# A selective-scan kernel whose channel picks contract 32 rows instead of 128

## What is computed

```python
def _mamba(x, in_proj_w, conv_w, conv_b, x_proj_w, dt_proj_w, dt_proj_b, A_log, Dvec, out_proj_w):
    xz = x @ in_proj_w.T
    xs, z = jnp.split(xz, 2, axis=-1)          # 128 inner channels each
    ...                                        # short convolution over tokens, silu
    dbc = xs @ x_proj_w.T
    dt = jax.nn.softplus(dbc[..., :DT_RANK] @ dt_proj_w.T + dt_proj_b)
    Bm = dbc[..., DT_RANK:DT_RANK + D_STATE]   # 16 states
    Cm = dbc[..., DT_RANK + D_STATE:]
    A = -jnp.exp(A_log)
    dA = jnp.exp(dt[..., None] * A)
    dBu = dt[..., None] * Bm[:, :, None, :] * xs[..., None]
    ...                                        # hs: h = dA * h + dBu along the tokens
    y = jnp.einsum('blds,bls->bld', hs, Cm) + xs * Dvec
    y = y * jax.nn.silu(z)
    return y @ out_proj_w.T
```

## Time and profile before

| | us |
|---|---|
| median of 3 runs | 6328.1 |
| lowest and highest | 6323.62 and 6338.3 |
| profiled execution, its own time | 6333.79 |
| its span, first to last instruction | 6332.1 |
| busy: PE | 4712.9 (74%) |
| busy: DVE | 4177.0 (66%) |
| busy: POOL | 3262.2 (52%) |
| busy: ACT | 3214.8 (51%) |
| granted TensorE clock, mean | 0.905 |

### The profile page before, as it was taken

One profiled execution on the slowest core, in us unless ns is written; L12 is line 12 of the kernel. 1 busy time (PEld: TensorE's weight loads), 2 busy tenths in 40 slices (PEclk: granted clock), 3 DMA queues, 4 the chain that ended last, 5 costly groups with the idle time before them and its releaser, 6 DMA issues. The chain is left out here.

```text
span 6332.1 us, 72725 instructions
## 1 busy us (share of the span) xinstructions
PE 4712.9 (74%) x22126; PEld 1875.5 (30%) x22126; DVE 4177.0 (66%) x6781; ACT 3214.8 (51%) x6875; POOL 3262.2 (52%) x2921
## 2 busy tenths in 40 slices
PE   4766887668876688766977669776797767977669
PEld 2322433214322143221432224322243223332233
DVE  3599635995359944599445994459834699346983
ACT  2555454554545555454554545445454454645545
POOL 1399203992149811498115980159701697017970
PEclk9899788997889988899888998889888998989989
DMA  3356133660335504365033650346413464135631
GB/s 86 82 139 140 26 78 74 147 144 14 88 85 138 135 10 94 79 149 124 18 91 91 139 117 21 87 99 146 102 25 83 108 141 98 28 80 122 140 85 28
DMA packets 205745, 582.54 MB, mean 92 GB/s; under 512 B 75652, under 2 KB 117892, under 8 KB 205188
## 3 DMA queue, kind: packets, MB, share of 16 engines
q1 hardware_dynamic: 205316, 577.47, 39.8%
HBM read 511.20 MB, written 66.20 MB: 91 GB/s over the span
## 5 line engine op out<-in xcount | busy, mean ns | idle before, releaser
L1065 POOL TENSOR_TENSOR hc<-hs,cb 128x448 f32<-128x448 f32 x1792 | 2029.2, 1146 | 329.1 <-DVE hs L1002 329.0
L1002 DVE TENSOR_TENSOR_SCAN hs<-dA,state,ps 128x448 f32<-128x448 f32 x1792 | 2036.4, 1137 | 13.8 <-ACT dA L965 13.8
L991 DVE TENSOR_TENSOR ps<-ps,bb 128x448 f32<-128x448 f32 x1792 | 1095.4, 611 | 309.4 <-PE ps L902 309.1
L952 ACT ACTIVATE state<-hs 128x1 f32<-128x1 f32 x1768 | 357.0, 202 | 1358.0 <-DVE hs L1002 1358.0
L902 PE MATMUL ps<-hx,pick 128*128 128x448 bf16 x2688 | 702.8, 376 | 413.2 <-DVE hs L1002 343.2
L902 PE MATMUL ps<-dux,pick 128*128 128x448 bf16 x2688 | 687.7, 370 | 364.6 <-DVE hs L1002 360.5
L537 POOL TENSOR_TENSOR sp<-hx,dA 128x448 f32<-128x448 f32 x56 | 59.9, 1069 | 1399.2 <-ACT dA L673 1399.2
L1412 DVE SCALAR_TENSOR_TENSOR dA<-ps,be,hs 128x448 f32<-128x448 f32 x224 | 153.2, 684 | 764.2 <-PE ps L1267 677.2
L1346 ACT ACTIVATE rz<-ps,be 128x448 f32<-128x448 f32 x896 | 540.8, 629 | 168.2 <-PE ps L1254 167.1
L1254 PE MATMUL ps<-u,we1s 128*128 128x448 bf16 x2688 | 614.3, 364 | 4.2 <-PEq L1093 4.2
L887 PE MATMUL ps<-hc,gather 128*32 128x448 f32 x3584 | 466.5, 594 | 144.9 <-POOL hc L1065 144.9
(11 more groups left out here) (186 smaller groups left out, 6697.6 us busy)
## 6 DMA issues: line engine op xcount, KB each, us to landing
rz<-dt_scratch SPq DMA_DIRECT2D x112, 896.0 KB, 6.4
x_all<-dt_scratch SPq DMA_DIRECT2D x112, 896.0 KB, 10.0
xn<-dt_scratch SPq DMA_DIRECT2D x112, 896.0 KB, 13.6
dtb<-dt_scratch SPq DMA_DIRECT2D x112, 896.0 KB, 13.3
zs<-h_scratch SPq DMA_DIRECT2D x174, 290.0 KB, 6.0
dt_scratch<-dtx SPq DMA_DIRECT2D x112, 224.0 KB, 1.9
h_scratch<-dA SPq DMA_DIRECT2D x168, 112.0 KB
u<-h_scratch SPq DMA_DIRECT2D x56, 336.0 KB, 4.1
```

Source lines behind the costliest of these rows:

```text
L952: A.activation(state[:, k % 2, i:i + 1], hs[:, n % RH, at:at + 1], ACT.Copy).then_inc(st_ok, 1)
L991: V.tensor_tensor(bank, bank, bb[:, k % 2, :], ALU.mult).then_inc(bu_ok, 1)
L1002: V.tensor_tensor_scan(rev(hs[:, n % RH, :], d), rev(dA[:, n % RA, :], d), rev(ps[BU[n % 3]][:, 0:CH], d), state[:, d, i:i + 1], ALU.mult, ...
L1065: P.tensor_tensor(hc[:, n % RC, :], hs[:, n % RH, :], cb[:, k % 2, :], ALU.mult).then_inc(hc_ok, 1)
```

## The change

A pick matmul now reads only the 32 lanes that hold its group's channels: stationary `pick[at, i % 4, :]` and moving `dux[k % 2][at, a, :]` with `at` the lanes 32 j to 32 j + 31, j = i // 4. Within such a block of 32 lanes the matrix depends on q = i % 4 alone, so four matrices take the place of sixteen, and each holds the same 32-row pattern in all four blocks. Results, output lanes, columns (128 stationary, 448 moving) and the number of matmuls stay as they were.

```diff
-        pick = sb("pick", [128, DS, 128], BF16)
+        pick8 = sb("pick8", [128, 4, 8])
+        pick = sb("pick", [128, 4, 128], BF16)
...
-                for i in range(DS):
-                    then(V.tensor_copy(pick[:, i, :].rearrange("p (s e) -> p s e", e=8),
-                                       ident[:, :].rearrange("p (j e q) -> p j q e", j=4, q=4)[:, i // 4, i % 4, :]
-                                       .unsqueeze(1).to_broadcast([128, DS, 8])))
+                for q in range(4):
+                    then(V.reduce_sum(pick8[:, q, :], ident[:, :].rearrange("p (j e q) -> p q e j", j=4, q=4)[:, q], axis=AX.X))
+                    then(V.tensor_copy(pick[:, q, :].rearrange("p (s e) -> p s e", e=8),
+                                       pick8[:, q, :].unsqueeze(1).to_broadcast([128, DS, 8])))
...
                         for a in range(3):
-                            last = nc.tensor.matmul(ps[BU[n % 3]][:, 0:CH], pick[:, i, :], top(dux[k % 2][:, a, :]),
+                            at = slice(32 * (i // 4), 32 * (i // 4) + 32)
+                            last = nc.tensor.matmul(ps[BU[n % 3]][:, 0:CH], pick[at, i % 4, :], top(dux[k % 2][at, a, :]),
                                                     start=(a == 0), stop=(a == 2))
```

## The result

The changed kernel takes 7308.6 us in the median of four runs (7298.0 to 7311.0), against 6333.2 before: a ratio of 1.154, 95% interval 1.152 to 1.156. It is slower by 975 us, clearly, and beyond the 7190 us at which the range ended. The direction and the place were forecast; the forecast growth, some 670 us, was a third too small.

What follows compares the result with a forecast made beforehand. VectorE sets the pace, TensorE is late at a few places. At 1.2 GHz a step grows from 27.1 to 34.0 us: 6328.1 + 707 (clock) - 44 (clock coming back) + 8 (start-up) = 6999, say 7000 us; range 6570 to 7190.

Steps and rivals of the forecast that it cites:

- the picks' own duration: Pick matmuls in the scan loop: contracting 32 rows instead of 128 makes them no shorter, 0 us.
- The preparation: VectorE's copies into the pick tile before the loop: any saving hides under GpSimd's power, so nothing gained.
- The clock: TensorE in the scan loop: empty rows don't count as activity, so 1.2 GHz through most of it, +707 us.
- The allowance for the clock coming back over skip and gather: Once per step: a quarter of the 1.58 us loss taken off in 112 steps, 44 us.
- A gather alone: Three per step at 1.2 GHz: the product behind the picks that follow is 0.89 us late each time.
- A preparation: dt, B, C matmuls between two pick groups, three per step: the product is 0.96 us late at 1.2 GHz.
- Skip and gather: Behind the gate, once per step: the product is 2.79 us late at 1.2 GHz, against 1.21 before.
- The upper bound: Every place at 1.2 GHz, picks after skip included, plus uncovered weight loads: 35.4 us a step, 7190 us.
- The sign that the prediction named: If the loop is far over 480 us: picks slow by themselves, over 1.4 us for three, from loads or drains.
- Same: Rival: busy time counts, not rows, so the loop's clock stays at 1.00; 6325 to 6330 us; 7%.
- faster: Rival: 32-row picks come out earlier, telling after skip and after the second gather; 45 us, 6283 us; 2%.
- Slower with the clock up: Rival: weight loads into the same 32 rows wait for the running matmul; 6373 to 6395 us; 3%.

Runs made afterwards that it cites:

- e1: Changed kernel plus useless 128-row filler matmuls on TensorE at the start of each image and behind pick groups without gather or preparation; 7122.9 us, ratio 1.123.
- e5: Changed kernel plus more 128-row fillers: bursts of 42 and 14 per image, 1 to 4 behind every other pick group; 6468.8 us, ratio 1.022.
- e2: Changed kernel with the fillers of e1, same number, places and columns, but over 32 rows instead of 128; 7444.5 us, ratio 1.175.
- e8: Kernel before, with its sixteen pick matrices and old preparation, only the picks reading 32 rows in every step; 7290.1 us, ratio 1.151.
- e4: Kernel before with its sixteen matrices, picks reading 32 rows in six of fourteen steps and 128 in the others; 6827.8 us, ratio 1.078.
- e3: Picks over 64 rows with eight pick matrices, instead of 32 rows with four as in the changed kernel; 7298.1 us, ratio 1.153 to the kernel before.
- e6: Kernel before, with 128-row picks, plus the same 128-row fillers as e5; 6278.3 us, ratio 0.991.

## Why the prediction was wrong in size and right in kind

**What bounds, and the picks' own duration: right.** In the stretches of e1 and e5 at 1.00 three narrow picks take 0.76 us, as full ones do (0.77). The Trainium skill's sentence "K=32 single mm = same time as K=128" (TensorE: Matmul & The Clock Gate, Why this matters for your kernels) holds here. Something that could run beside the narrow picks existed all the same, on other rows and into another bank: the fillers of e2.

**The preparation: right**, by e8, the first scan at 282 us in both, and the idle time of 8.21 us.

**The clock: right.** 0.51 over the block, within the "0.5 to 0.6" named, and the wait of the product went where it was looked for. The inference from the earlier trace rows is confirmed for 32 rows by the pair e1 and e2, and by e4: rows left empty count less. That such a pick counts for a quarter is not shown; by that rule 64 rows would count half, and they lost the clock as 32 do (e3). That empty columns don't count either was tested by no run. The allowance for the clock coming back over skip and gather, 44 us, was too large: it was up there for a part of the wait in 32 of 112 steps, and the product is 3.26 us late there in the mean against 3.36 in the median, some 11 us in all.

**The price of the places at 1.2 GHz: here the sum failed.** This is the step of the prediction that failed: the mechanism stands, its three prices of a late product were too low, because they were read from places where the clock was already rising or where full-row picks stood around, and a change of height was put at nothing in the forecast. A step was put at 34.0 us and is 37.1. The 3.1 us are all in the three terms:

- *A gather alone, 0.89 us, is 1.24; three of them, 1.05 us.* The row behind it, the product at 2085.93 in the earlier trace rows, stands where the clock was already coming back. The gather ran at 1.2 GHz, but the picks behind it took 0.96 us there, not 1.30. The prediction allowed for this behind skip and not here. 0.89 + 0.34 = 1.23.
- *A preparation, 0.96 us, is 1.45; three of them, 1.47 us.* The row has full-row picks around it. e4 has both cases, one step apart, and the low clock up to 2221.41 us. With narrow picks, the product is idle for 1.34 us:

```profile
2180.91 1.30 PE L903 MATMUL ps<-dux,pick 32*128 32x448 bf16 x3
...
2182.13 0.50 PEld L864 LDWEIGHTS ps<-u,wdt 128*128 128x128 f32 x2 [0.73 <-issue]
2182.14 1.86 PE L864 MATMUL ps<-u,wdt 128*128 128x448 f32 x2
...
2183.93 2.42 PE L903 MATMUL ps<-dux,pick 32*128 32x448 bf16 x6
...
2185.26 0.63 DVE L992 TENSOR_TENSOR ps<-ps,bb 128x448 f32<-128x448 f32 x1 [1.34 <-PE ps L903]
```

  and with full-row picks 0.76 us:

```profile
2217.99 1.30 PE L903 MATMUL ps<-hx,pick 128*128 128x448 bf16 x3
...
2218.72 0.70 PEld L864 LDWEIGHTS ps<-u,wdt 128*128 128x128 f32 x2 [0.23 <-issue]
2219.09 1.70 PE L864 MATMUL ps<-u,wdt 128*128 128x448 f32 x2
...
2220.58 1.75 PE L903 MATMUL ps<-hx,pick 128*128 128x448 bf16 x6
...
2221.77 0.63 DVE L992 TENSOR_TENSOR ps<-ps,bb 128x448 f32<-128x448 f32 x1 [0.76 <-PE ps L903]
```

  From picks to preparation 1.23 us against 1.10, from preparation to picks 1.79 against 1.49: going to the preparation and back costs 0.13 + 0.30 = 0.43 us. (The idle times differ by more, 0.58 us, because with full rows the clock rose during the last of the picks before the product.) Of the 0.30, 0.14 lie between the preparation and the picks and 0.16 inside the preparation, between its two matmul records, which start 0.91 us apart behind narrow picks and 0.74 behind full ones. Before the change there was none of this, since picks and preparations both used all 128 rows. The rows of the weight loads (PEld) show what is different: behind full-row picks the load for the preparation starts 0.37 us ahead of its matmul, under the last pick; behind narrow picks it starts with its matmul. The prediction named the drain of the Trainium skill (TensorEngine Tiling (Array Packing), Key Properties) and gave it no value in the sum. The trace agrees with the page in that each such change costs time; whether the time is a drain, or the load that no longer lies under a matmul, it can't tell apart. Further, the picks before a preparation are already late there, so that the little slack of the old row (0.06 us) was gone: 0.96 + 0.43 + 0.06 = 1.45.
- *Skip and gather, 2.79 us, is 3.36; once a step, 0.57 us.* The 0.5 us for picks at the low clock was known and was put into the upper bound only, not into the forecast, though the same text said that the clock would be low there.

1.05 + 1.47 + 0.57 = 3.09 us a step. By block of 14 steps: the forecast had 473.1 us, 14 x 3.09 = 43.3 make it 516.4, and the last step saves three preparations at 1.45 us and not at 0.96, which leaves 515.0. A block measures 506.7, because the first step and the last two of an image are shorter than that and the clock comes back now and then (the 11 us). So a block is 33.6 us over the forecast's, eight are 269 us, and the 44 us of the allowance, whose true size is now in the block, come on top: 7000 + 269 + 44 = 7313 us, against 7309 measured.

**The upper bound** failed for the same reason. It had 0.9 us a step for weight loads left uncovered at nine pick groups; what came is 1.3 us (3 x 0.43) at the three preparations, where the load starts with its matmul, and 1.05 us behind the lone gathers, for which it had nothing. The sign that the prediction named for a loop far over 480 us, three picks that take over 1.4 us, did not come: they take 1.30.

**The rivals.** "Same" is out, and so is "faster". "Slower with the clock up" exists but is small: e5 shows 1.5 us a step, and only with a full-row filler behind each pick group; e1 shows 0. So the time that the prediction gave it, 6373 to 6395 us, is tested by no run without fillers.

## What to carry to other kernels

Before narrowing a matmul to fewer rows because "only those are used", ask what it saves (here nothing, 0.76 us for three either way, unless another matmul on other rows runs beside them, as the fillers of e2 do) and what the engine's clock will make of it; a TensorE that isn't the bound may still be the one whose clock sets the pace. A kernel that waits at a few places for TensorE, with the granted clock between the levels, can gain from useless full-size matmuls in TensorE's idle time (here 0.9%), if they go where there is slack and the clock is up; at the low clock they cost. And when a cost is read from a rare row, check the clock of every instruction in the chain, not just of the first, and whether the neighbours will have the shape that they have in that row.

## What the runs showed of the hardware

- One program, e1, settles at either clock: steps of 27.2 us at 1.00 and of 44.5 us at 0.50, several in a row each, before it changes over.
- A change between 32-row and 128-row matmuls costs 0.10 us in each direction at 2.4 GHz (e5 against e6); at 1.2 GHz 0.13 us to 128 rows and 0.14 us to 32 (e4). Behind such a change the preparation's own two matmul records lie further apart as well, by 0.16 us at 1.2 GHz (e4) and 0.10 at 2.4 (0.48 against 0.38, e1 against the kernel before). A change between 64 and 128 rows costs as much at 1.2 GHz (e3). Between the gathers, 32 columns wide, and narrow picks the starts are 1.65 us apart, as they were with full ones at that clock.
- Matmuls on the rows 0 to 31 run at the same time as matmuls on other rows: 0.01 us from start to start, six in the time of three (e2).
- Rows decide over the clock at the same busy share: 91% busy at 1.00 with fillers over 128 rows (e1), 92% at 0.50 with fillers over 32 (e2).
- 64 rows instead of 128 lose the clock as fully as 32 do in this loop (0.52 and 0.51).
